# A sequence layer and a product-key expert layer on one core: the one-hots of the second half of a step stand behind the next step's weights, and the turned lists have two buffers

## The chip, the cores and the metric

The kernel runs on one core of one Trainium2 chip. The metric is the device time of one execution in microseconds (us). Five engines work side by side: TensorE (matmuls and transposes, into PSUM), VectorE, ScalarE, GpSimd, and SyncE, which here only starts transfers. Each runs its own instructions in the order in which they are written, and waits for semaphores that the others raise.

## The reference

The input is 4 sequences of 1024 tokens with 128 features. First layer: four projections, softplus, sigmoid and tanh, a scan along the sequence, a gate, an output projection, residual and layer norm. Second layer, cut to what matters here (8 heads, 32 keys, TOPK = 8, 1024 experts):

```python
q = (xn @ w_q.T).reshape(b, n, 2, h, kd).transpose(2, 0, 1, 3, 4)
sim = jnp.einsum('pbnhd,hkpd->pbnhk', q, keys)
s, i = jax.lax.top_k(sim, k)
sx, sy = (s[0], s[1])
ix, iy = (i[0], i[1])
all_scores = (sx[..., :, None] + sy[..., None, :]).reshape(b, n, h, k * k)
all_idx = (ix[..., :, None] * nk + iy[..., None, :]).reshape(b, n, h, k * k)
scores, pk = jax.lax.top_k(all_scores, k)
idx = jnp.take_along_axis(all_idx, pk, axis=-1)
w_down = key_in[idx]
w_up = key_out[idx]
o = jnp.einsum('bnd,bnhkd->bnhk', inputs, w_down)
o = jax.nn.gelu(o, approximate=False) * jax.nn.softmax(scores, axis=-1)
return jnp.einsum('bnhk,bnhkd->bnd', o, w_up)
```

`xn` is a batch norm of `inputs` over all tokens. A residual and a layer norm follow.

## The kernel before

The first layer takes the first fifth of the span and is not touched. The second is a loop of 16 steps (NS) of 256 tokens. It gathers no expert weights. All 1024 experts are evaluated for all tokens by dense matmuls; the weights of the chosen experts are scattered into a dense matrix P (tokens by experts) by small matmuls of one-hots; gelu times P goes through a dense output matmul. The chosen expert is coded as a coarse index of 64 (NI) and a fine index of 16 (NJ).

For the tokens of step m the work is this, by functions:

- `scores(m)` (TensorE, line 837): similarities of two tiles; `sims_out(m)` (ScalarE, line 383) evacuates them, `normed` (line 375) makes the input of a later step.
- `greatest(m)` (VectorE, line 606): the 8 greatest of each row. `candidate_sums(m)` (GpSimd, lines 239 to 248) makes 20 candidate sums and differences. `indices(m)` (VectorE, line 614) finds the indices, `top_sums(m)` (line 620) the 8 greatest candidates. `candidate_codes(m)` and `over_eighth(m)` (GpSimd, lines 253 to 270) make codes and the comparison with the eighth. ScalarE makes exponentials (`exps`, `low_halves`) and signs (`signs`, line 399).
- One step later `pack`, `pick`, `weights_and_codes` (VectorE, lines 627 to 654) pick the 8 codes and weights of the step. `pack` waits for the signs.
- `halves` (GpSimd, lines 277 and 279) splits the weights in a high and a low half in f16, `convert` (ScalarE, line 404) copies the codes. Together they are the four lists.
- `lists_turned(m)` (TensorE, line 844) transposes the lists into a PSUM bank, `lists_out(m)` (ScalarE, line 409) evacuates them to `listsT`.
- `hots_of(m, hf)` (VectorE, lines 666 to 673) makes the one-hots of half `hf` of the step from `listsT` in four instructions, a block of its own for each half. The second is the longest (line 669, 4096 elements a partition).
- `scatter(m, hf)` (TensorE, line 857): 256 small matmuls with their weight loads, from the one-hots of the half; `p_out(m, hf)` (ScalarE, line 417) evacuates the result.
- `weigh(m)` (GpSimd, line 286, four instructions): P times gelu. `experts_in(q)` (TensorE, line 867) and `gelus(q)` (ScalarE, line 423) stand in odd steps only and serve two steps. `experts_out(m)` (TensorE, line 880): the output matmul.
- `residual`, `scales` (VectorE), `spread2`, `norm_out` (ScalarE): the last layer norm of four tiles, once in two steps: `residual` and `spread2` (with a table load for the square root) in odd steps, `scales` and `norm_out` in even ones.

The order on each engine is written out by hand in the loops over m at the end of each block. In iteration m, VectorE runs greatest(m), pack to weights of m - 1, indices(m), top_sums(m), then both blocks of one-hots of m - 1, with `residual` or `scales` between the two. TensorE runs scatter(m - 2, second half), lists_turned(m - 1), scores(m + 1), experts_in in odd steps, scatter(m - 1, first half), experts_out(m - 3). ScalarE follows TensorE: p_out of the second half, lists_out, sims_out, normed, gelus, spread2, signs, norm_out, p_out of the first half. GpSimd runs candidate_sums(m), halves(m - 1), weigh(m - 3), candidate_codes(m), over_eighth(m).

`listsT` is one buffer: lists_out(m) waits until both blocks of one-hots of the step before are done. The functions that the diff touches:

Of the kernel before, what the change touches and what calls it, by code (L numbers as in the profile page):

```python
# [6 lines left out]
ACT = mybir.ActivationFunctionType  # L7
AX_X = mybir.AxisListType.X
F32 = mybir.dt.float32
F16 = mybir.dt.float16  # L10
# [4 lines left out]
P = 128  # L15
# [8 lines left out]
def seqffn_kernel(nc, x, w_in, w_select, w_gate, w_out, w_delta, log_a, gamma, beta, w_q, keys,  # L24
# [16 lines left out]
    NS = T // 2  # L41
# [9 lines left out]
    with ExitStack() as ctx:  # L51
        def sb(name, shape, dt=F32):
            return ctx.enter_context(nc.sbuf_tensor(name, shape, dt))
# [54 lines left out]
        wk = sb("wk", [P, RH, TOPK])  # L108
        codes = sb("codes", [P, 2, 2 * SL], U16)
        lists = sb("lists", [P, 4, 2 * SL], F16)  # L110
        listsT = sb("listsT", [P, 4, P], F16)


        XW, YW = P * NI // 2, P * NJ // 2
# [29 lines left out]
        b_lists = bank(7)[:, 0:256].bitcast(F16)  # L144
# [14 lines left out]
        s = {n: sem(n) for n in names}  # L159
# [5 lines left out]
        def wait(eng, name, value):  # L165
            if value <= 0:
                return
            eng.wait_ge(s[name], value)
# [134 lines left out]
        def _(act):  # L303
# [92 lines left out]
            def signs(m):  # L396
                wait(act, "dt_done", m + 1)
                wait(act, "hi_done", m)
                act.activation(sgn[:, :], above[:, :, :].rearrange("p h c -> p (h c)"), ACT.Sign).then_inc(s["sgn_done"], 1)
# [5 lines left out]

            def lists_out(m):
                wait(act, "lists_mm", m + 1)
                wait(act, "hot_done", m * 2)
                act.activation(listsT[:, :, :].rearrange("p f t -> p (f t)"), b_lists, ACT.Copy).then_inc(s["lists_evac"], 1)  # L409

            def p_out(m, hf):
                wait(act, "p_mm", m * 2 + hf + 1)
# [6 lines left out]
            def gelus(q):  # L419
                wait(act, "y2_mm", q * 2 - 2)  # L420
                for r in range(JR):
                    wait(act, "g_mm", q * JR + (r + 1))
                    act.activation(gl[:, (2 * q) % 4:(2 * q) % 4 + 2, 2 * r:2 * r + 2, :].rearrange("p m j w -> p j m w"),  # L423
                                   b_g[r % 2].rearrange("p (j m w) -> p j m w", j=2, m=2), ACT.Gelu).then_inc(
                                       s["gelu_done"], 1)
# [32 lines left out]
            for m in range(NS + 1):  # L458
                if m < NS:
                    exps(m)  # L460
                if m >= 1:
                    convert(m - 1)
                if m < NS:
                    low_halves(m)
                if m == NS:
                    lists_out(NS - 1)
                if m >= 2:
                    p_out(m - 2, 1)
                if 1 <= m < NS:
                    lists_out(m - 1)  # L470
                if m + 1 < NS:
                    sims_out(m + 1)
                if m + 2 < NS:
                    normed(m + 2)
                if m % 2 and m < NS:
                    gelus(m // 2)
                if m >= 5 and m % 2:
                    spread2(m // 2 - 2)
                if m < NS:
                    signs(m)  # L480
                if m >= 6 and m % 2 == 0:
                    norm_out(m // 2 - 3)
                if m >= 1:
                    p_out(m - 1, 0)
# [8 lines left out]
        def _(dve):  # L493
# [147 lines left out]
            def weights_and_codes(m):  # L641
                wait(dve, "conv_done", m)
                wait(dve, "picked_done", m + 1)
                dve.tensor_copy(exk16, picked16[:, :, :, 0]).then_inc(s["exk_done"], 1)
                dve.tensor_scalar(codes[:, 0, :], picked16[:, 0, :, 1], NE - NJ, None, ALU.bitwise_and)
                wait(dve, "exk_done", m + 1)
                dve.reduce_sum(zsum[:, :], exk[:, :, :], AX_X).then_inc(s["z_done"], 1)
                dve.tensor_scalar(codes[:, 1, :], picked16[:, 0, :, 1], NJ - 1, None,
                                  ALU.bitwise_and).then_inc(s["codes_done"], 1)
                wait(dve, "z_done", m + 1)  # L650
                dve.reciprocal(zinv[:, :], zsum[:, :]).then_inc(s["zinv_done"], 1)
                wait(dve, "zinv_done", m + 1)
                wait(dve, "wlo_done", m)
                dve.scalar_tensor_tensor(out=wk[:, :, :], in0=exk[:, :, :], scalar=W_SCALE,
                                         in1=zinv[:, :].unsqueeze(2).to_broadcast([P, RH, TOPK]), op0=ALU.mult,
                                         op1=ALU.mult).then_inc(s["wk_done"], 1)

            def hots_of(m, hf):
                at = slice(32 * hf, 32 * hf + 32)

                def spread(f, n):
                    v = listsT[:, f, 64 * hf:64 * hf + 64].rearrange("p (g s) -> p g s", s=2)
                    return v.unsqueeze(2).to_broadcast([P, 32, n, 2])

                wait(dve, "lists_evac", m + 1)
                dve.tensor_tensor(hoty[:, at], iota[:, NI:].unsqueeze(1).to_broadcast([P, 32, NJ, 2]),  # L666
                                  spread(1, NJ), ALU.is_equal).then_inc(s["hoty_done"], 1)
                wait(dve, "p_mm", m * 2 - 1 + hf)
                dve.tensor_tensor(hotx[:, at], iota[:, 0:NI].unsqueeze(1).to_broadcast([P, 32, NI, 2]),  # L669
                                  spread(0, NI), ALU.is_equal)  # L670
                wait(dve, "hoty_done", m * 2 + hf + 1)
                dve.tensor_tensor(hotw[:, 0, at], hoty[:, at], spread(2, NJ), ALU.mult)  # L672
                dve.tensor_tensor(hotw[:, 1, at], hoty[:, at], spread(3, NJ), ALU.mult).then_inc(s["hot_done"], 1)  # L673

            def residual(q):
                wait(dve, "out_done", q)
                wait(dve, "y2_mm", q * 2 + 2)
                dve.tensor_tensor(zf.rearrange("p (m e) d -> p m e d", e=2), y2.rearrange("p e m d -> p m e d"),
                                  x1[:, q * CH:(q + 1) * CH, :].rearrange("p (m e) d -> p m e d", e=2),
                                  ALU.add).then_inc(s["zf_done"], 1)  # L680
                wait(dve, "zf_done", q + 1)
                for t in range(CH):
                    end = dve.bn_stats(st2[:, t, :], zf[:, t, :])
                end.then_inc(s["st2_done"], 1)
                wait(dve, "st2_done", q + 1)
                for t in range(CH):
                    end = dve.bn_aggr(mv2[:, t, :], st2[:, t, :])
                end.then_inc(s["mv2_done"], 1)

            def scales(q):  # L690
                wait(dve, "sd2", q + 1)
                dve.reciprocal(rstd2[:, :], rstd2[:, :]).then_inc(s["rstd2_done"], 1)
                wait(dve, "rstd2_done", q + 1)
                dve.scalar_tensor_tensor(out=nmr2[:, :], in0=mv2[:, :, 0], scalar=-1.0, in1=rstd2[:, :],
                                         op0=ALU.mult, op1=ALU.mult).then_inc(s["nmr2_done"], 1)

            for m in range(NS + 1):
                if m < NS:
                    greatest(m)
                if m >= 1:  # L700
                    pack(m - 1)
                    pick(m - 1)
                    weights_and_codes(m - 1)
                if m < NS:
                    indices(m)
                    top_sums(m)
                if m >= 1:
                    hots_of(m - 1, 0)
                    if m >= 5 and m % 2:
                        residual(m // 2 - 2)  # L710
                    if m >= 6 and m % 2 == 0:
                        scales(m // 2 - 3)
                    hots_of(m - 1, 1)

            def last_residual(u):
                n = slice(2 * u, 2 * u + 2)
# [36 lines left out]
        def _(pe):  # L753
# [64 lines left out]
            for r in range(ROWS):  # L818
                p, h = r // H, r % H
# [63 lines left out]

            scores(0)
            for m in range(NS + 1):
                if m == NS:
                    lists_turned(NS - 1)
                if m >= 2:
                    scatter(m - 2, 1)
                if 1 <= m < NS:  # L890
                    lists_turned(m - 1)
                if m + 1 < NS:
                    scores(m + 1)
                if m % 2 and m < NS:
                    experts_in(m // 2)
                if m == NS:
                    wait(pe, "lists_evac", NS)
                    experts_out(NS - 3)
                if m >= 1:
                    scatter(m - 1, 0)  # L900
                if 3 <= m < NS:
                    wait(pe, "lists_evac", m)
                    experts_out(m - 3)
# [28 lines left out]
```

## Time and profile before

| | |
|---|---|
| median of 3 runs | 532.36 us (530.75 to 534.48) |
| the profiled execution | 531.46 us, span 529.7 us |
| mean granted TensorE clock | 0.768 |
| PE (TensorE matmuls) busy | 369.5 us, 70% |
| DVE (VectorE) busy | 444.1 us, 84% |
| ACT (ScalarE) busy | 236.2 us, 45% |
| POOL (GpSimd) busy | 220.0 us, 42% |
| the chain that ended last, by engine | PE 52%, DVE 20%, issue 17%, ACT 8% |

The span is what the trace covers; the execution's own time is 1.8 us longer. PE stands for TensorE's matmuls and PEld for its weight loads, which overlap them. The chain is followed back from the last instruction, at each step to what released it. "issue" is time in which an engine waited for nothing that the profile shows.

### The profile page before, as it was taken

Reading aid. Unit: us, or ns where it says so; the run is one execution under the profiler, and the core shown is the slowest. Engines: PE = TensorE matmul, PEld = TensorE weight load, DVE = VectorE, ACT = ScalarE, POOL = GpSimd, SP = SyncE. Lnnn points to the kernel's source line nnn. Section 1 sums busy time; section 2 is a strip of 40 time slices with the busy share of each in tenths; the row PEclk is TensorE's granted clock in tenths of the full one; section 3 lists DMA queues with packets and bytes.
Section 4 is the critical chain, followed back from the end, with each engine's and each line's share of the span. In section 5 each row is a group of like instructions: output and inputs, shape, how many; then the busy total and the mean of one; then the engine's idle time right before and its main releaser. Section 6 shows DMA issues by size and latency. Waiting matters only on the chain.

```text
span 529.7 us, 24223 instructions
## 1 busy us (share of the span) xinstructions
PE 369.5 (70%) x10097; PEld 270.4 (51%) x10097; DVE 444.1 (84%) x2770; ACT 236.2 (45%) x371; POOL 220.0 (42%) x311
## 2 busy tenths in 40 slices
PE   5686786418537775786777787847976876778856
PEld 2233474114434555464736484726464656556855
DVE  1537899699999969898999699989998997998643
ACT  3967804426514532463346235632644372345212
POOL 1042420144348751616283428435252747082630
PEclk9989965759655876898778668876886796588878
DMA  8700000000000000000000000000000000000001
GB/s 236 165 0 2 1 1 0 1 1 2 4 2 5 3 2 4 3 4 4 24 2 4 4 24 3 4 22 5 2 5 24 5 3 4 22 4 2 24 6 41
DMA packets 7661, 8.95 MB, mean 17 GB/s; under 512 B 896, under 2 KB 6912, under 8 KB 7424
## 3 DMA queue, kind: packets, MB, share of 16 engines
q1 hardware_dynamic: 6976, 7.34, 5.1%
q8 instruction: 79, 1.29, 1.0%
q14 instruction: 30, 0.25, 0.1%
q10 hardware_dynamic: 576, 0.07, 0.1%
HBM read 5.31 MB, written 2.10 MB: 14 GB/s over the span
## 4 chain that ended last, share of the span: by engine, by line
PE 52%; DVE 20%; issue 17%; ACT 8%; DMA 1%; SPq 0%; ACTq 0%; DVEq 0%
PE psum L880 17%; PE psum L857 16%; PE psum L867 9%; PE psum L837 5%; PE psum L776 4%; DVE arena L669 3%; DVE idx L614 3%; DVE arena L525 2%; DVE x L575 2%; ACT L423 1%; DVE vals L606 1%; DVE arena L673 1%; DVE arena L666 1%; DVE arena L672 1%; DVE picked L638 1%
## 5 line engine op out<-in xcount | busy, mean ns | idle before, releaser
L857 PE MATMUL psum<-arena 64*64 64x16 f16 x8192 | 93.8, 182 | 91.5 <-issue 70.0
L857 PEld LDWEIGHTS psum<-arena 64*64 64x64 f16 x8192 | 87.7, 120 | 110.0 <-issue 104.8
L880 PE MATMUL psum<-ko,arena 64*128 64x128 f32 x1024 | 91.2, 355 | 3.6 <-issue 3.6
L417 ACT ACTIVATE arena<-psum 128x1024 f32<-128x1024 f32 x32 | 32.8, 1024 | 134.0 <-PE psum L857 134.0
L880 PEld LDWEIGHTS psum<-ko,arena 64*128 64x128 f32 x1024 | 88.0, 267 | 4.2 <-issue 3.9
L239 POOL TENSOR_TENSOR cand<-vals 128x128 f32<-128x128 f32 x16 | 13.2, 824 | 169.1 <-DVE vals L606 169.1
L614 DVE FIND_INDEX8 idx<-vals,sims 128x8 uint32<-128x32 f32 x512 | 82.7, 185 | 0.0
L286 POOL TENSOR_TENSOR arena<-arena 128x512 f32<-128x512 f32 x60 | 77.8, 1331 | 4.2 <-ACT arena L417 4.2
L669 DVE TENSOR_TENSOR arena<-iota,listsT 128x4096 f16<-128x4096 f16 x32 | 74.9, 2341 | 0.0
L867 PE MATMUL psum<-x1T,trn 128*64 128x256 f32 x512 | 62.8, 400 | 8.7 <-ACT arena L423 8.7
L837 PE MATMUL psum<-msim,xn 128*128 128x512 f32 x64 | 54.9, 1008 | 4.9 <-ACT xn L375 4.9
L867 PEld LDWEIGHTS psum<-x1T,trn 128*64 128x64 f32 x512 | 33.9, 143 | 43.9 <-ACT arena L423 20.7
L606 DVE MAX8 vals<-sims 128x8 f32<-128x32 f32 x512 | 49.1, 173 | 3.7 <-ACT sims L383 3.5
L666 DVE TENSOR_TENSOR arena<-iota,listsT 128x1024 f16<-128x1024 f16 x32 | 23.2, 724 | 26.6 <-ACT listsT L409 26.6
L423 ACT ACTIVATE arena<-psum 128x512 f32<-128x512 f32 x64 | 37.4, 597 | 17.2 <-PE psum L867 17.1
L638 DVE MAX8 picked<-words 128x8 f32<-128x20 f32 x512 | 42.8, 165 | 1.7
L776 PE MATMUL psum<-arena,trn 128*128 128x512 f32 x64 | 34.6, 674 | 10.1 <-ACT arena L343 8.8
L614 DVE MATCH_VALUE_LOAD idx<-vals,sims 128x8 f32 x512 | 36.8, 72 | 0.0
L383 ACT ACTIVATE sims<-psum 128x512 f32<-128x512 f32 x32 | 19.0, 596 | 27.6 <-PE psum L837 27.5
L259 POOL TENSOR_TENSOR code<-ixf,iyf 128x128 f32<-128x128 f32 x16 | 30.3, 1891 | 1.3
L837 PEld LDWEIGHTS psum<-msim,xn 128*128 128x128 f32 x64 | 17.6, 301 | 22.3 <-issue 19.5
L776 PEld LDWEIGHTS psum<-arena,trn 128*128 128x128 f32 x64 | 12.2, 215 | 26.5 <-issue 18.6
(113 smaller groups left out, 529.5 us busy)
## 6 DMA issues: line engine op xcount, KB each, us to landing
x<-in_L_attn_x_dram SPq DMA_DIRECT2D x8, 256.0 KB, 4.7
out_dram<-nat SPq DMA_DIRECT2D x7, 256.0 KB, 2.3
ko<-in_L_ffn_key_out_dram SPq DMA_DIRECT2D x2, 512.0 KB, 9.5
nat<-in_L_ffn_key_in_dram SPq DMA_DIRECT2D x2, 256.0 KB, 8.0
nat<-in_L_ffn_keys_dram SPq DMA_DIRECT2D x2, 128.0 KB, 5.4
out_dram<-nat SPq DMA_DIRECT2D x2, 128.0 KB, 1.7
nat<-in_L_attn_W_delta_dram SPq DMA_DIRECT2D x1, 64.0 KB, 2.8
nat<-in_L_attn_W_in_dram SPq DMA_DIRECT2D x1, 64.0 KB, 2.7
```

The lines of the kernel that those rows point to most:

```text
L286: pool.tensor_tensor(gl[:, m % 4, js], pn[:, m % 3, js], gl[:, m % 4, js], ALU.mult).then_inc(s["a_done"], 1)
L417: act.activation(dst, src, ACT.Copy, scale=1.0 / W_SCALE).then_inc(s["p_evac"], 1)
L423: act.activation(gl[:, (2 * q) % 4:(2 * q) % 4 + 2, 2 * r:2 * r + 2, :].rearrange("p m j w -> p j m w"), b_g[r % 2].rearrange("p (j m w) - ...
L606: end = dve.max(vals[:, p, t * H + h, :], sims[:, m % 2, t, r, :])
L614: end = dve.max_index(idx[:, p, t * H + h, :], vals[:, p, t * H + h, :], sims[:, m % 2, t, r, :])
L638: end = dve.max(picked[:, w, r, :], words[:, w, r, :])
L669: dve.tensor_tensor(hotx[:, at], iota[:, 0:NI].unsqueeze(1).to_broadcast([P, 32, NI, 2]), spread(0, NI), ALU.is_equal)
L776: pe.matmul(to, trn[:, n, :], xT[:, k], start=True, stop=True).then_inc(s[done], 1)
L837: pe.matmul(b_sim[t], xn[:, t], msim[:, :], start=True, stop=True).then_inc(s["sim_mm"], 1)
L857: end = pe.matmul(psum[64 * e:64 * e + 64, at:at + NJ], hotx[rows, g, :, e], hotw[rows, part, g, :, e], start=(part == 0), stop=(part == 1))
L867: end = pe.matmul(b_g[r % 2][64 * e:64 * e + 64, b * SW:(b + 1) * SW], trn[:, 9 + r, 64 * b:64 * b + 64], tokens[:, e], start=True, stop=True)
L880: end = pe.matmul(y2[:, e, m % 2] if m < NS - 1 else y_last[:, e], gl[rows, m % 4, j, :], ko[rows, j, :], start=(j == 0), stop=(j == NJ - 1))
```

## The change

VectorE's second block of one-hots of a step moves: it now stands one iteration later, behind pack, pick and weights of the following step and ahead of indices. `scales` stands behind it, `residual` behind the first block. TensorE turns the lists ahead of the second-half scatter, ScalarE evacuates the lists ahead of that scatter's result. `listsT` gets two buffers, so that lists_out(m) waits only for the one-hots of step m - 2. On ScalarE the signs stand ahead of `spread2`.

```diff
-        listsT = sb("listsT", [P, 4, P], F16)
+        listsT = sb("listsT", [P, 2, 4, P], F16)
...
             def lists_out(m):
                 wait(act, "lists_mm", m + 1)
-                wait(act, "hot_done", m * 2)
-                act.activation(listsT[:, :, :].rearrange("p f t -> p (f t)"), b_lists, ACT.Copy).then_inc(s["lists_evac"], 1)
+                wait(act, "hot_done", (m - 1) * 2)
+                act.activation(listsT[:, m % 2].rearrange("p f t -> p (f t)"), b_lists, ACT.Copy).then_inc(s["lists_evac"], 1)
...
                 if m < NS:
                     low_halves(m)
-                if m == NS:
-                    lists_out(NS - 1)
+                if m >= 1:
+                    lists_out(m - 1)
                 if m >= 2:
                     p_out(m - 2, 1)
-                if 1 <= m < NS:
-                    lists_out(m - 1)
                 if m + 1 < NS:
                     sims_out(m + 1)
                 if m + 2 < NS:
                     normed(m + 2)
                 if m % 2 and m < NS:
                     gelus(m // 2)
+                if m < NS:
+                    signs(m)
                 if m >= 5 and m % 2:
                     spread2(m // 2 - 2)
-                if m < NS:
-                    signs(m)
...
-                    v = listsT[:, f, 64 * hf:64 * hf + 64].rearrange("p (g s) -> p g s", s=2)
+                    v = listsT[:, m % 2, f, 64 * hf:64 * hf + 64].rearrange("p (g s) -> p g s", s=2)
...
                     pack(m - 1)
                     pick(m - 1)
                     weights_and_codes(m - 1)
+                if m >= 2:
+                    hots_of(m - 2, 1)
+                if m >= 6 and m % 2 == 0:
+                    scales(m // 2 - 3)
                 if m < NS:
                     indices(m)
                     top_sums(m)
                 if m >= 1:
                     hots_of(m - 1, 0)
-                    if m >= 5 and m % 2:
-                        residual(m // 2 - 2)
-                    if m >= 6 and m % 2 == 0:
-                        scales(m // 2 - 3)
-                    hots_of(m - 1, 1)
+                if m >= 5 and m % 2:
+                    residual(m // 2 - 2)
+            hots_of(NS - 1, 1)
...
             for m in range(NS + 1):
-                if m == NS:
-                    lists_turned(NS - 1)
+                if m >= 1:
+                    lists_turned(m - 1)
                 if m >= 2:
                     scatter(m - 2, 1)
-                if 1 <= m < NS:
-                    lists_turned(m - 1)
                 if m + 1 < NS:
                     scores(m + 1)
```

## Rows read from the trace of the kernel before

**Rows 1.** Waits: engine and line, waited for: us in total, times, longest us.
```profile
DVE arena L666 <- ACT listsT L409: 26.6, 9, 5.1
...
PE psum L857 <- DVE arena L673: 18.0, 7, 6.0
```

**Rows 2.** Timeline of TensorE: start us, us, work, [idle before and releaser]; pairs' ends.
```profile
150.49 2.05 PE L857 MATMUL psum<-arena 64*64 64x16 f16 x130 [5.97 <-DVE arena L673]
...
169.72 1.45 PE L867 MATMUL psum<-x1T,trn 128*64 128x256 f32 x6
...
178.38 1.72 PE L857 MATMUL psum<-arena 64*64 64x16 f16 x184
...
481.37 1.77 PE L857 MATMUL psum<-arena 64*64 64x16 f16 x190
```

**Rows 3.** Timeline of TensorE, one pair of steps, 333 to 384 us.
```profile
333.31 1.72 PE L857 MATMUL psum<-arena 64*64 64x16 f16 x185
...
353.67 1.09 PE L857 MATMUL psum<-arena 64*64 64x16 f16 x110 [2.46 <-DVE arena L673]
357.02 1.89 PE L857 MATMUL psum<-arena 64*64 64x16 f16 x128 [2.26 <-issue]
...
366.81 1.62 PE L857 MATMUL psum<-arena 64*64 64x16 f16 x173
...
371.50 0.40 PE L844 MATMUL psum<-ident,lists 128*128 128x128 f16 x4
...
383.80 0.37 PE L857 MATMUL psum<-arena 64*64 64x16 f16 x23
```

**Rows 4.** Timeline of ScalarE in the same pair.
```profile
333.43 0.60 ACT L423 ACTIVATE arena<-psum 128x512 f32<-128x512 f32 x1 [0.27 <-PE psum L867]
...
335.54 0.45 ACT L399 ACTIVATE sgn<-above 128x320 f32<-128x320 f32 x1
...
347.86 1.02 ACT L417 ACTIVATE arena<-psum 128x1024 f32<-128x1024 f32 x1 [5.91 <-PE psum L857]
348.78 0.59 ACT L409 ACTIVATE listsT<-psum 128x512 f16<-128x512 f16 x1
```

**Rows 5.** Timeline of VectorE in the same pair.
```profile
336.08 0.94 DVE L627 SCALAR_TENSOR_TENSOR words<-sgn,code 128x640 uint16<-128x640 f32 x1 [0.28 <-issue]
...
340.88 0.29 DVE L654 SCALAR_TENSOR_TENSOR wk<-exk,zinv 128x128 f32<-128x128 f32 x1
...
346.25 1.37 DVE L620 MAX8 top<-cand 128x8 f32<-128x20 f32 x16
349.40 0.72 DVE L666 TENSOR_TENSOR arena<-iota,listsT 128x1024 f16<-128x1024 f16 x1 [1.79 <-ACT listsT L409]
...
353.72 0.69 DVE L666 TENSOR_TENSOR arena<-iota,listsT 128x1024 f16<-128x1024 f16 x1
...
357.73 3.07 DVE L606 MAX8 vals<-sims 128x8 f32<-128x32 f32 x32
360.72 0.87 DVE L627 SCALAR_TENSOR_TENSOR words<-sgn,code 128x640 uint16<-128x640 f32 x1
```

**Rows 6.** Timeline of GpSimd in the same pair, behind the weights.
```profile
341.30 0.29 POOL L277 CAST lists<-wk 128x128 f16<-128x128 f32 x1 [2.77 <-DVE wk L654]
341.67 0.43 POOL L279 TENSOR_TENSOR lists<-wk,lists 128x128 f16<-128x128 f32 x1
342.06 4.95 POOL L286 TENSOR_TENSOR arena<-arena 128x512 f32<-128x512 f32 x4
```

**Rows 7.** Timelines of VectorE and GpSimd, start-up and a later odd step.
```profile
122.15 0.76 DVE L666 TENSOR_TENSOR arena<-iota,listsT 128x1024 f16<-128x1024 f16 x1
...
123.05 2.36 POOL L264 TENSOR_TENSOR code<-ixf,iyf 128x64 f32<-128x64 f32 x1
...
127.05 0.68 DVE L666 TENSOR_TENSOR arena<-iota,listsT 128x1024 f16<-128x1024 f16 x1
...
270.05 4.31 POOL L259 TENSOR_TENSOR code<-ixf,iyf 128x128 f32<-128x128 f32 x1
```

## The prediction

> **What bounds the kernel now.** I read the busy shares first, then the waits, then the timeline of each engine over one pair of steps. VectorE is busy for 84% of the span, but the waits name only one real hole in it: 26.6 us in nine waits of line 666 for the turned lists [rows 1]. TensorE waits 18.0 us in seven waits for a finished hot block (line 673) [rows 1]; one of them, 5.97 us, is in the start-up [rows 2], so the other six are 2.0 us each.
>
> The step loop repeats in pairs, because the expert matmuls (line 867) and their gelus stand only in odd steps. The first scatter after them starts at 178.38 us in the first full pair and at 481.37 us in the last [rows 2]: six pairs in 303.0 us, 50.5 us each. I take the pair from 333.31 to 383.80 (50.49 us) as the pattern [rows 3]. In it two rings can be seen:
>
> - TensorE's ring: the second-half scatter starts at 366.81, the turning of the lists only follows at 371.50 [rows 3]. ScalarE must then first empty the scatter (347.86) and only after that the lists (348.78) [rows 4], so VectorE begins the next first half 1.79 us late, at 349.40 [rows 5], and TensorE waits for it until 353.67 [rows 3]. This is what the change goes for.
> - VectorE's ring has almost no slack: the last gelu of the pair starts at 333.43 and the signs, behind the square root, at 335.54 [rows 4]; pack starts at 336.08 [rows 5].
>
> TensorE without its one 2.0 us wait would need 48.5 us a pair, so nothing that only frees VectorE can give more than about 2.0 x 6 + 6.0 = 18 us.
>
> **What the change removes.** The lists are turned ahead of the second-half scatter and evacuated ahead of p_out, and a second buffer lets that happen while the old lists are still read. The lists then stand ready well before indices and top sums end, so the wait of line 666 goes: I cost the list waits at 0 after the change (the cover is 6.5 us of indices and top sums). The signs no longer stand behind the square root and its table load: pack may start 1.2 us after the expert matmuls end instead of 2.77 us (0.1 us to the last gelu, 0.6 us of it, 0.5 us as now between signs and pack: 333.43, 335.54, 336.08 against 333.31) [rows 3 to 5]. The second buffer itself issues nothing. No DMA moves.
>
> **What the change adds.** The second-half block of one step now stands between the next step's weights and its indices, and its scatter comes directly after it. Everything that TensorE does after the lists waits for that block. The new ring, from the end of the expert matmuls to the end of the next, by the durations of the rows:
>
> 1. gelu and signs: 1.2 us.
> 2. pack, pick, weights: 336.08 to 341.1 (line 654 starts at 340.88, 0.2 us between starts) [rows 5]: 5.0 us.
> 3. second-half block: 353.72 to 357.73 = 4.0 us when undisturbed [rows 5].
> 4. scales: 0.3 us (the gap between the two blocks beyond 4.0).
> 5. indices and top sums: 341.1 to 347.55 (346.25 + 1.37, less 0.07 overlap) [rows 5]: 6.45 us.
> 6. first-half block: 4.0 us undisturbed.
> 7. greatest: 357.73 to 360.72 = 3.0 us [rows 5]; its similarities are there, since their matmuls run beside the block of point 6.
> 8. pack, pick, weights again: 4.95 us.
> 9. second-half block again: 4.0 us; to TensorE 0.1 us.
> 10. scatter, similarities, expert matmuls: 366.81 to 383.80 [rows 3] = 17.0 us.
>
> The sum is 50.0 us, against 50.5 us now. So even with every block undisturbed the ring only changes its shape: the 2 us that TensorE loses today at line 857 it goes on losing, because points 1 to 6 (21.0 us) reach the first-half scatter later than 353.67 - 333.31 = 20.36 us [rows 3]. VectorE's freed time turns into a wait at pack: its own work is about 47.3 us a pair (50.5 less its waits of about 3), and the ring holds it at signs for the rest.
>
> **The price of the neighbours.** The blocks will not be undisturbed. Now the second-half block runs while GpSimd waits. After the change it starts 0.2 us after line 654 starts, while GpSimd starts line 277 at 0.42 us (341.30 against 340.88), then line 279, then four products of 4.95 us together [rows 5, 6]. What such neighbours do is seen in the start-up: a first-half block from 122.15 took 4.9 us to the next block's start at 127.05 instead of 4.0, and line 264 of GpSimd took 2.36 us beside line 669 [rows 7]. In the other pattern GpSimd gets nothing until the block is over: line 259 took 4.31 us from 270.05 [rows 7]. The Trainium skill, "Trainium Architecture — The Big Picture", "What this means for kernel authors", says that VectorE and GpSimd share a port pair under an exclusive lock, not a split bandwidth. By that rule alone the block would stay at 4.0 us and GpSimd's halves would come after it; the trace has that pattern in rows 7, and also the one in which VectorE pays.
>
> Bounds per pair. Lowest: nobody is disturbed, 50.0 us. GpSimd held: the halves (0.3 + 0.4 us and their gaps) and the turned lists (0.4 us) come after the block, in front of its scatter, +1.4 us in point 9: 51.4 us. VectorE disturbed: the product behind the halves is longer (4.95 / 4 = 1.24 us) than the line of the start-up, so a second-half block may reach 5.4 us, and the first-half one 4.9 us: 53.7 us. I take 4.9 us for the second-half blocks, the measured disturbed block, and half of its surplus for the first-half one (GpSimd's codes are delayed by the products and overlap it in part): 50.0 + 0.9 + 0.9 + 0.45 = 52.25 us, that is +1.75 x 6 = +10.5 us over the six pairs.
>
> **Start-up.** The first-half block of step 1 is done at 150.4 now and then too, as VectorE has no wait there. Greatest, weights and the second-half block follow: 150.4 + 3.0 + 4.95 + 4.9 = 163.3, then scatter and similarities of 4.7 + 3.7 us: 171.7, where the expert matmuls now start at 169.72 [rows 2]. With half a microsecond for the disturbed block of step 0: +2.5 us. **Tail.** After 481.37 the weights of the last step and the moved block end 1.2 + 5.0 + 4.9 = 11.1 us later; TensorE reached that scatter 11.9 us later, so 0.
>
> Sum: 531.46 us of the profiled execution + 10.5 + 2.5 = 544.5 us. The median shown is 0.9 us above that execution, so 545 us.
>
> **The rivals.**
>
> - *Nothing to see.* GpSimd gives way cheaply, or the disturbed blocks fall where TensorE is late anyway (the first-half scatter from 353.67 and the experts' output together take 13.1 us, more than the 12.0 us of points 7 to 9). Then -0.5 x 6 + 1 to +0.7 x 6: 530 to 537 us. For it: several pairs have such long scatters. Against it: point 9 is the wait of TensorE in all others.
> - *Faster.* TensorE's scatters hold issue gaps, as the 2.26 us before 357.02 [rows 3], that no engine causes. If the new wait in front of the second-half scatter lets the instructions gather, point 10 shrinks by up to 2.0 us, and with undisturbed blocks a pair takes 48.0 to 49.5 us: -1 to -2.5 a pair, 517 to 526 us. It decides from 49.6 us a pair down. Against it: this very scatter follows a wait of 2.46 us and still gets no further than 110 matmuls before its gap [rows 3].
> - *The halves held and the block undisturbed*, 51.4 us a pair: +5.4 + 2 = 539 us. It is the lower end of my own case.
>
> **Chances.** One per cent, about what can be told from no change, is 5.3 us. My case (new ring, disturbed by GpSimd), 538 to 556 us: 0.61. Nothing to see: 0.25. Faster: 0.14. The range reaches from inside the faster case, 527, to the full disturbed sum: 53.7 us gives +19 us and +3.5 us at the start, 554; I end it at 555. My own case has the range 538 to 555. Faster by over 1%: 0.14; within 1%: 0.25; slower: 0.61.
>
> **What would show it.** Line 666 no longer waits for line 409. Line 627 waits about 2 us in every even step, and what ended that wait is the sign of line 399, right behind the last gelu. TensorE waits for line 673 twice a pair, at both scatters, in all some 25 to 35 us instead of 18.0. Line 279 grows from 0.43 us to over 1 us, or lines 666 to 673 from 4.0 to about 4.9 us a block. A pair takes 52 us. I am wrong if pairs fall under 50 us; then either pack does not wait for the gelus or point 10 is shorter than 17.0 us.

## The result: 566.15 us, slower by 6.6%

The changed kernel takes 566.15 us (median of 4 runs, 564.82 to 567.88) against 533.36 us of the kernel before beside it; the ratio is 1.0657, 95% interval 1.0602 to 1.0713. It was forecast slower, but 545 us and at most 555. The new ring that was forecast is there, but the price put on GpSimd's neighbourhood in it, and on the start, was too low.

### The profile after

Shares of the page after (busy us, share of the span of 566.1 us, instructions):

```profile
PE 379.6 (67%) x10097; PEld 277.9 (49%) x10097; DVE 482.1 (85%) x2770; ACT 235.9 (42%) x371; POOL 280.4 (50%) x311
```

VectorE has the same instructions and is busy 38 us longer, GpSimd 60 us longer. So the same work takes longer, which no wait for a semaphore shows. On GpSimd alone that need not cost time: in e1 below it is busy 267.3 us at the time of the kernel before. The waits after (engine, line, waited for: us in total, times, longest):

```profile
ACT listsT L409 <- PE psum L844: 47.4, 16, 4.8
...
PE psum L857 <- DVE arena L671: 38.6, 17, 4.2
...
DVE words L625 <- issue: 25.7, 7, 7.0
```

VectorE's wait for the turned lists [rows 1] has gone from the list. In its place VectorE waits at pack (line 625, "issue", 25.7 us in 7 waits), and TensorE's waits for a finished block went from 18.0 us in 7 to 38.6 us in 17.

One pair of steps on TensorE after, which answers to [rows 3]. Lines above 600 on VectorE stand two lower after the change: line 671 is line 673 of the kernel before, 667 is 669.

```profile
352.92 1.72 PE L857 MATMUL psum<-arena 64*64 64x16 f16 x185
...
363.16 0.40 PE L844 MATMUL psum<-ident,lists 128*128 128x128 f16 x4
364.70 2.19 PE L857 MATMUL psum<-arena 64*64 64x16 f16 x243 [1.14 <-DVE arena L671]
...
377.17 1.67 PE L857 MATMUL psum<-arena 64*64 64x16 f16 x110 [4.10 <-DVE arena L671]
```

TensorE now waits at both scatters of the even step. Its pairs end at 186.89, 240.20, 295.15, 352.92, 407.04, 462.05 and 516.54 us: 54.9 us each, where it was 50.5 [rows 2]. VectorE in the same pair, which answers to [rows 5]:

```profile
354.08 0.92 DVE L625 SCALAR_TENSOR_TENSOR words<-sgn,code 128x640 uint16<-128x640 f32 x1 [5.38 <-issue]
...
359.06 0.69 DVE L664 TENSOR_TENSOR arena<-iota,listsT 128x1024 f16<-128x1024 f16 x1
359.66 2.38 DVE L667 TENSOR_TENSOR arena<-iota,listsT 128x4096 f16<-128x4096 f16 x1
361.96 0.91 DVE L670 TENSOR_TENSOR arena<-arena,listsT 128x1024 f16<-128x1024 f16 x1
362.80 1.75 DVE L671 TENSOR_TENSOR arena<-arena,listsT 128x1024 f16<-128x1024 f16 x1
364.47 0.17 DVE L690 RECIPROCAL rstd<-rstd 128x4 f32<-128x4 f32 x1
364.67 1.02 DVE L692 SCALAR_TENSOR_TENSOR nmr<-mv,rstd 128x4 f32<-128x4 f32 x1
...
372.06 0.75 DVE L664 TENSOR_TENSOR arena<-iota,listsT 128x1024 f16<-128x1024 f16 x1
...
375.79 1.23 DVE L671 TENSOR_TENSOR arena<-arena,listsT 128x1024 f16<-128x1024 f16 x1
376.95 3.06 DVE L604 MAX8 vals<-sims 128x8 f32<-128x32 f32 x32
```

And GpSimd beside it, which answers to [rows 6]:

```profile
359.28 0.62 POOL L277 CAST lists<-wk 128x128 f16<-128x128 f32 x1 [8.44 <-DVE wk L652]
359.98 2.35 POOL L279 TENSOR_TENSOR lists<-wk,lists 128x128 f16<-128x128 f32 x1
362.29 5.84 POOL L286 TENSOR_TENSOR arena<-arena 128x512 f32<-128x512 f32 x4
```

I read this as the two engines taking turns. Line 279 (0.43 us before) ends 0.3 us after line 667; line 671 (0.68 us undisturbed) takes 1.75 us while the first product of line 286 runs; and line 692, four elements a partition, takes 1.02 us instead of 0.16 beside the next product. That the products do this to line 671 is tested in e4. The second-half block takes 5.41 us (359.06 to 364.47), the scales 1.15 us with their gaps (to 365.62), the first-half block 4.89 us (372.06 to 376.95). From block to block these lengths repeat within 0.03 us, in every step from 3 to 14.

### The profile page after: what moved, and what is told of

The parts are those of the page before. It is cut to its first block, busy times and chain, and to the rows that moved or that the text cites. A ratio compares the mean times of both kernels' runs of the same rounds, so it can differ in the third digit from the quotient of the medians.

```text
span 566.1 us, 24222 instructions
## 1 busy us (share of the span) xinstructions
PE 379.6 (67%) x10097; PEld 277.9 (49%) x10097; DVE 482.1 (85%) x2770; ACT 235.9 (42%) x371; POOL 280.4 (50%) x311
## 4 chain that ended last, share of the span: by engine, by line
DVE 47%; PE 28%; issue 15%; ACT 8%; DMA 1%; SPq 0%; DVEq 0%; POOL 0%; ACTq 0%
DVE idx L612 7%; PE psum L857 7%; DVE picked L636 7%; DVE arena L667 5%; DVE arena L671 5%; PE psum L837 5%; PE psum L880 5%; PE psum L867 5%; DVE vals L604 4%; PE psum L776 4%; DVE arena L670 3%; DVE arena L664 2%; DVE words L625 2%; DVE arena L523 2%; DVE top L618 2%
## 5 line engine op out<-in xcount | busy, mean ns | idle before, releaser
L857 PE MATMUL psum<-arena 64*64 64x16 f16 x8192 | 99.2, 185 | 110.6 <-issue 70.6
L857 PEld LDWEIGHTS psum<-arena 64*64 64x64 f16 x8192 | 93.3, 125 | 130.3 <-issue 128.3
L286 POOL TENSOR_TENSOR arena<-arena 128x512 f32<-128x512 f32 x60 | 92.7, 1575 | 0.0
L880 PE MATMUL psum<-ko,arena 64*128 64x128 f32 x1024 | 90.2, 353 | 3.2 <-issue 3.2
L667 DVE TENSOR_TENSOR arena<-iota,listsT 128x4096 f16<-128x4096 f16 x32 | 78.4, 2450 | 0.0
L239 POOL TENSOR_TENSOR cand<-vals 128x128 f32<-128x128 f32 x16 | 11.6, 723 | 92.3 <-DVE vals L604 92.3
L867 PEld LDWEIGHTS psum<-x1T,trn 128*64 128x64 f32 x512 | 33.9, 143 | 43.3 <-ACT arena L423 20.4
L671 DVE TENSOR_TENSOR arena<-arena,listsT 128x1024 f16<-128x1024 f16 x32 | 46.1, 1442 | 0.0
L277 POOL CAST lists<-wk 128x128 f16<-128x128 f32 x16 | 9.3, 581 | 73.6 <-DVE wk L652 73.6
L423 ACT ACTIVATE arena<-psum 128x512 f32<-128x512 f32 x64 | 37.4, 597 | 17.5 <-PE psum L867 17.4
L776 PE MATMUL psum<-arena,trn 128*128 128x512 f32 x64 | 36.0, 699 | 10.1 <-ACT arena L343 8.8
L279 POOL TENSOR_TENSOR lists<-wk,lists 128x128 f16<-128x128 f32 x16 | 35.7, 2231 | 1.3
L625 DVE SCALAR_TENSOR_TENSOR words<-sgn,code 128x640 uint16<-128x640 f32 x16 | 14.3, 895 | 25.7 <-issue 25.7
L264 POOL TENSOR_TENSOR code<-ixf,iyf 128x64 f32<-128x64 f32 x16 | 35.8, 2236 | 0.0
## 6 DMA issues: line engine op xcount, KB each, us to landing
ko<-in_L_ffn_key_out_dram SPq DMA_DIRECT2D x2, 512.0 KB, 10.1
```

Source lines behind the costliest of these rows:

```text
L286: pool.tensor_tensor(gl[:, m % 4, js], pn[:, m % 3, js], gl[:, m % 4, js], ALU.mult).then_inc(s["a_done"], 1)
L776: pe.matmul(to, trn[:, n, :], xT[:, k], start=True, stop=True).then_inc(s[done], 1)
L857: end = pe.matmul(psum[64 * e:64 * e + 64, at:at + NJ], hotx[rows, g, :, e], hotw[rows, part, g, :, e], start=(part == 0), stop=(part == 1))
L867: end = pe.matmul(b_g[r % 2][64 * e:64 * e + 64, b * SW:(b + 1) * SW], trn[:, 9 + r, 64 * b:64 * b + 64], tokens[:, e], start=True, stop=True)
L880: end = pe.matmul(y2[:, e, m % 2] if m < NS - 1 else y_last[:, e], gl[rows, m % 4, j, :], ko[rows, j, :], start=(j == 0), stop=(j == NJ - 1))
```

## The experiments

Each ratio is to the kernel before, run beside it on the same chip. "Pair" is the mean of the six pairs, read as in [rows 2]; the second and the last end are given where the start matters.

**e1: the lists' part alone.** Edits to the kernel before: `listsT` doubled and `lists_out` with the changed wait, and on TensorE (on ScalarE alike)

```diff
-                if m == NS:
-                    lists_turned(NS - 1)
+                if m >= 1:
+                    lists_turned(m - 1)
                 if m >= 2:
                     scatter(m - 2, 1)
-                if 1 <= m < NS:
-                    lists_turned(m - 1)
```

> The part of the change that concerns the lists, alone: two buffers, lists turned ahead of the second-half scatter and evacuated ahead of its result; both blocks of one-hots stay together on VectorE, the signs stay behind the square root. Theory (the new ring through the moved block is guilty, the lists' part is good): line 666 no longer waits for the lists (26.6 us before), a pair of steps falls from 50.5 to 48.5 to 49.5 us, 519 to 527 us in all. Rival (TensorE's new order is itself the cost): 545 us or more. Rival (the freed wait only moves): 530 to 535 us.

533.34 us, ratio 1.0021 (0.9981 to 1.0061): no difference. But the pairs fell to 49.55 us, and VectorE's waits for the lists from 26.6 us in nine to one of 3.2 us; 5 us were lost ahead of the pairs. TensorE in iteration 3 of e1:

```profile
154.43 1.88 PE L855 MATMUL psum<-arena 64*64 64x16 f16 x126 [1.84 <-issue]
163.33 0.79 PE L842 MATMUL psum<-ident,lists 128*128 128x128 f16 x4 [7.02 <-issue]
164.05 1.88 PE L855 MATMUL psum<-arena 64*64 64x16 f16 x125
```

The scatter at 164.05 had its one-hots long before, but stands behind the lists of the next step, which VectorE had not made yet. Before, it began at 157.7 us. The forecast "545 us or more" for TensorE's order falls; so does my 519 to 527.

**e2: the moved block alone**, lists and signs as before, one buffer.

```diff
                     weights_and_codes(m - 1)
+                if m >= 2:
+                    hots_of(m - 2, 1)
+                if m >= 6 and m % 2 == 0:
+                    scales(m // 2 - 3)
...
-                    hots_of(m - 1, 1)
+            hots_of(NS - 1, 1)
```

> The other part alone: the second-half block stands behind the next step's weights (scales behind it, residual behind the first block); one buffer for the turned lists, the old order of lists, scatter and signs on TensorE and ScalarE. Theory: the moved block makes the ring, so this is at least as slow as the whole change, 563 to 575 us, with a pair at 54.5 to 56.5 us. Rival (the order of the lists and of the signs is guilty): 530 to 540 us.

578.92 us, ratio 1.0884 (1.0826 to 1.0942), pair 56.75 us. The move alone costs 47 us; the lists' and the signs' part give 12 us of that back in the whole change. The move is the guilty part. With one buffer and the old order VectorE also waits for the lists here, 10.1 us in seven waits.

**e3: the ring cut.** The changed kernel with the signs ahead of the gelus on ScalarE:

```diff
+                if m < NS:
+                    signs(m)
                 if m % 2 and m < NS:
                     gelus(m // 2)
-                if m < NS:
-                    signs(m)
```

> The changed kernel with the signs of a step ahead of its gelus on ScalarE, so that pack of the next step no longer waits for the expert matmuls. Theory (a ring gelus, signs, pack, block, ..., block, scatter, expert matmuls of 54.9 us): the ring is cut, VectorE's wait of about 5 us at pack goes, a pair takes what VectorE's own work takes, 49.5 to 51.5 us, and the whole 533 to 546 us. Rival (TensorE's waits and lower clock, or the port between VectorE and GpSimd by itself, make the time): above 558 us.

553.08 us, ratio 1.0388 (1.0342 to 1.0433), between theory and rival. The line of pack's waits is gone, as the theory has it, but the pair takes 52.8 us and the start lost 7 us: the gelus of step 1 had to wait for its signs, and the first pair began at 138.35 instead of 131.63 us. By the second pair some 2 us of that are left: from the first similarities to it e3 takes 91.1 us, the changed kernel 88.7, and e11, which takes this fault out, 89.0.

**e4: the products held.** The changed kernel with

```diff
                 if m >= 3:
+                    wait(pool, "hot_done", (m - 1) * 2)
                     weigh(m - 3)
```

> The changed kernel with one wait more on GpSimd: the four products of weigh start only when the second-half block that stands beside them is done. Theory (GpSimd's products lengthen the block, twice in the ring): line 671 falls from 1.75 us to 1.25 or less in the second-half blocks, the block from 5.4 to 4.4 to 4.9 us, a pair by 1 to 2 us, the whole to 552 to 561 us. Rival (the lengthening costs nothing, since something else is late): 564 to 568 us.

556.00 us, ratio 1.0466 (1.04 to 1.0532), pair 53.5 us: as the theory says, with the block a little shorter than it had it. A second-half block of e4:

```profile
349.36 0.68 DVE L665 TENSOR_TENSOR arena<-iota,listsT 128x1024 f16<-128x1024 f16 x1
349.96 2.38 DVE L668 TENSOR_TENSOR arena<-iota,listsT 128x4096 f16<-128x4096 f16 x1
352.26 0.91 DVE L671 TENSOR_TENSOR arena<-arena,listsT 128x1024 f16<-128x1024 f16 x1
353.09 0.68 DVE L672 TENSOR_TENSOR arena<-arena,listsT 128x1024 f16<-128x1024 f16 x1
```

The last instruction (line 672 here, 671 of the changed kernel) is back at 0.68 us, and the block is 4.34 us. Adding a wait made the changed kernel 10 us faster.

**e7: line 279 left out too** (the low halves of the weights are set to zero once, and what waited for line 279 waits for line 277), products held as in e4.

```diff
                 pool.tensor_copy(lists[:, 2, :], flat).then_inc(s["whi_done"], 1)
-                wait(pool, "whi_done", m + 1)
-                pool.tensor_tensor(lists[:, 3, :], flat, lists[:, 2, :], ALU.subtract).then_inc(s["wlo_done"], 1)
```

> The changed kernel with GpSimd's neighbours of the second-half block nearly taken away: line 279 is left out (the low halves of the weights are zero, so the weights are coarser), and weigh waits for the block. Theory (GpSimd's access beside the block lengthens it from 4.0 to 5.4 us, twice a ring): block 4.0 to 4.3 us, pair 52 to 53 us, whole 544 to 554 us. Rival (e4 took all that there is to take): 555 to 558 us.

550.58 us, ratio 1.04 (1.0331 to 1.047), pair 53.2 us, just above the range given. The total lies in its range, but its ratio is not clear of e4's (1.0466), so that leaving out line 279 gains more time is not shown; its block shows what line 279 did. Every instruction but one has the undisturbed length:

```profile
347.18 0.69 DVE L664 TENSOR_TENSOR arena<-iota,listsT 128x1024 f16<-128x1024 f16 x1
347.78 2.38 DVE L667 TENSOR_TENSOR arena<-iota,listsT 128x4096 f16<-128x4096 f16 x1
350.08 0.68 DVE L670 TENSOR_TENSOR arena<-arena,listsT 128x1024 f16<-128x1024 f16 x1
350.69 0.68 DVE L671 TENSOR_TENSOR arena<-arena,listsT 128x1024 f16<-128x1024 f16 x1
351.29 0.16 DVE L690 RECIPROCAL rstd<-rstd 128x4 f32<-128x4 f32 x1
351.48 1.25 DVE L692 SCALAR_TENSOR_TENSOR nmr<-mv,rstd 128x4 f32<-128x4 f32 x1
```

The block is 4.10 us; the products, now released right there, meet the scales instead (1.25 us).

**e8: e3 and e4 together**, both edits as above.

> The changed kernel with the edits of e3 and e4 together: signs ahead of the gelus, products held until the block is done. Theory (two causes that add: the ring is worth 2.2 us a pair and the products 1.4 us a pair): VectorE without waits, pair 51 to 52 us, whole 539 to 549 us. Rival (the two hide each other): the time of e3, 550 to 555 us.

541.48 us, ratio 1.022 (1.0159 to 1.0281), pair 50.6 us. The two causes add: 2.7% (e3) and 1.9% (e4), 4.4% together. The start has the fault of e3 (first pair from 139.34 us).

**e11 and e10: the signs first from iteration 3 on**, in e11 alone, in e10 with the products held.

```diff
+                if 3 <= m < NS:
+                    signs(m)
                 if m % 2 and m < NS:
                     gelus(m // 2)
-                if m < NS:
+                if m < 3:
                     signs(m)
```

> The changed kernel with the signs first from iteration 3 on and nothing else: the ring cut, the neighbours on the port left. Theory: pairs of 52.8 us as in e3, 541 to 547 us; against the changed kernel's 566 us the ring is worth 19 to 25 us, the rest is VectorE's own lengthened work. Rival (e3's time was not that of its start): 550 us or more.

e11: 547.82 us, ratio 1.0282 (1.0229 to 1.0336), pair 52.2 us; the median is 0.8 us above the range given, far from the rival.

> The changed kernel with both edits of e8, the signs first only from iteration 3 on (in e3 and e8 the first gelus waited for the signs of step 1 and the first scatter behind the expert matmuls began 9 us late). Theory (ring and port together are the whole loss): pairs of 50.5 us as in e8, 529 to 536 us, no more than 1% over before. Rival (something else costs too): 538 us or more.

e10: 540.50 us, ratio 1.0155 (1.0103 to 1.0208), pair 50.7 us. The pairs came as expected, the total did not: the rival's number holds. Of its 8 us over the kernel before, the trace has 1 us in the six pairs, 1 us behind them and 5.3 us ahead of them: the second pair starts at 183.64, where it was 178.38 [rows 2].

**e5 and e6: more of the lists' part.** e5 has e1's edits with the old order up to iteration 2, e6 the signs ahead of the gelus as well.

> The lists' part alone as in e1, but the first three iterations keep the old order (in e1 the second scatter of step 1 stood behind the lists of step 2 and began at 164.1 instead of 157.7 us, and the expert matmuls 5 us later). Theory: the 5 us of the start-up come back and the pairs of 49.5 us stay (50.5 before), 524 to 529 us. Rival (the shorter pairs of e1 were paid for by the late start, the work only spreads): 531 to 534 us.

> As e5, and the signs of a step ahead of its gelus on ScalarE. Theory: pack's waits (21.5 us in e1) go, VectorE is ready sooner and TensorE, with 48.5 us of its own a pair, is the only bound: 519 to 526 us. Rival (TensorE bounds already, VectorE's wait costs nothing): the time of e5 within 2 us.

e5: 532.21 us, ratio 1.0029 (0.999 to 1.0067). I had put the border one iteration too early: the late scatter stands in iteration 3, and the first pair again took 54.1 us. e6: 540.81 us, ratio 1.0193 (1.0132 to 1.0253), pair 49.5 us as in e5, and the gelus of step 1 late. Pack's waits (22.1 us in e5) went, and VectorE waited for the lists instead (36.3 us in 8 waits): in this order of VectorE the time of a pair does not go through pack. What e6 lost, it lost at the start.

**e9: the lists early from iteration 4 on**, the blocks where they were.

```diff
+                if m >= 4:
+                    lists_turned(m - 1)
                 if m >= 2:
                     scatter(m - 2, 1)
-                if 1 <= m < NS:
+                if 1 <= m < 4:
                     lists_turned(m - 1)
```

> The lists' part alone, early from iteration 4 on instead of 3 (e5 still had the late scatter of step 1, which stands in iteration 3: its first pair took 54.1 us, 49.4 before). Theory: the start-up is that of before and the six pairs stay at 49.5 us (50.5 before): 523 to 528 us, 1% under before. Rival (TensorE bounds, and what the pairs gain at the start of the loop goes back): 529 to 533 us.

526.91 us, ratio 0.992 (0.9885 to 0.9954): 0.8% faster than the kernel before, a small gain, but its interval is clear of 1. Pair 49.7 us, first pair 48.5. Here the lists go ahead and the scatter behind them waits for nobody:

```profile
336.10 0.40 PE L844 MATMUL psum<-ident,lists 128*128 128x128 f16 x4
336.42 2.52 PE L857 MATMUL psum<-arena 64*64 64x16 f16 x243
...
341.75 3.78 PE L837 MATMUL psum<-msim,xn 128*128 128x512 f32 x4
345.46 1.67 PE L857 MATMUL psum<-arena 64*64 64x16 f16 x110
```

The first-half scatter at 345.46, 19.3 us behind the expert matmuls (326.20), has no wait where the kernel before had 2.46 us and 20.4 us [rows 3]. In all of e9 TensorE waits for a block once:

```profile
PE psum L857 <- DVE arena L673: 6.5, 1, 6.5
```

**e12: the signs' part alone**, signs ahead of spread2 in the kernel before.

> The third part of the change alone: the kernel before with the signs ahead of spread2 on ScalarE. Theory (in the kernel before TensorE and the lists set the pair, pack has slack behind it): pack starts 1.6 us earlier in even steps, the wait of line 666 for the lists grows by as much, and the time stays, 528 to 536 us. Rival (pack is on the path there too): 1.6 us off each of 6 pairs, 520 to 525 us.

530.44 us, ratio 0.9994 (0.9944 to 1.0044): no difference, as expected. The waits for the lists did not grow (22.1 us in 8 here), so that detail of the theory is not borne out.

## Why the prediction was wrong

**Right: what it does.** The waits for the lists went; pack waits for the signs behind the last gelu (354.08 against 352.92, 1.16 us where I had 1.2); TensorE waits at both scatters (38.6 us in all, where I had 25 to 35). e3, e8 and e11 show that the ring exists: with it cut, pack's waits are gone and the ratio falls from 1.0657 to 1.0282, 3.75% or 20 us. e4 shows that GpSimd beside the second-half blocks lengthens them and that this reaches the end. e2 shows that it is the moved block and not the order of the lists.

**Argued, not shown: the bare ring costs nothing.** Points 1 to 10 with undisturbed blocks gave 50.0 us. No run has the ring without GpSimd beside it: e7 comes nearest, with 53.2 us a pair, and still has the first-half block at 4.88 us and the scales at 1.37. What can be checked are the pieces. Measured pieces of the same ring in the pair from 352.92 to 407.04, in the order of the points: 1.16, 4.98, 5.41, 1.15, 6.44, 4.89, 2.98, 4.90, 5.42, 0.35, 16.44, sum 54.1 us. Every piece on VectorE that meets none of GpSimd's long instructions is within 0.06 us of what I had; the last two, TensorE's, are 0.25 us more and 0.6 us less in this pair.

**Wrong: the step "The price of the neighbours".** It is a matter of size: the forecast has this cost, and too little of it. I took 4.9 us for the second-half blocks and half of the surplus for the first-half one, a middle between bounds, and had the whole reason for the upper bound in hand: the product behind the halves is 1.24 us long and must be let through. Measured, with what it was short by in a pair:

- second-half block 5.41 us, not 4.9: 2 x 0.5 = 1.0 us;
- first-half block 4.89 us, not 4.45: 0.45 us; GpSimd's codes start when the indices are done and always meet it;
- scales 1.15 us, not 0.3: 0.85 us, in none of the bounds. I had costed the moved line of four elements by its length without neighbours, though it too has two inputs in SBUF and stands beside the products;
- point 10, scatter to the end of the expert matmuls: 17.5 us in the mean of six (16.4 to 20.3), not 17.0: 0.5 us. The chosen pair was a fast one: in the kernel before the mean of six was already 17.3 us.

52.25 + 2.8 = 55.0 us; measured 54.9. Over six pairs I forecast +10.5 us; it was +26.7.

The whole price was in the trace before, in its last block, which the forecast did not use. There a block met the products of line 286 and took 7.24 us (499.15 to 506.39), up to 1.1 us more for one instruction:

```profile
498.27 0.68 DVE L673 TENSOR_TENSOR arena<-arena,listsT 128x1024 f16<-128x1024 f16 x1
...
499.06 0.16 DVE L694 SCALAR_TENSOR_TENSOR nmr<-mv,rstd 128x4 f32<-128x4 f32 x1
499.15 0.68 DVE L666 TENSOR_TENSOR arena<-iota,listsT 128x1024 f16<-128x1024 f16 x1
499.75 3.37 DVE L669 TENSOR_TENSOR arena<-iota,listsT 128x4096 f16<-128x4096 f16 x1
503.04 1.76 DVE L672 TENSOR_TENSOR arena<-arena,listsT 128x1024 f16<-128x1024 f16 x1
504.72 1.75 DVE L673 TENSOR_TENSOR arena<-arena,listsT 128x1024 f16<-128x1024 f16 x1
```

```profile
499.15 8.44 POOL L286 TENSOR_TENSOR arena<-arena 128x512 f32<-128x512 f32 x4 [4.16 <-ACT arena L417]
```

**TensorE's clock is not the cause.** The mean granted clock over the six pairs was 0.73 after and 0.77 before, so e3's rival has to be weighed. TensorE was busy 229.7 us in them after and 225.0 us before, so a slower clock can account for about 4.6 of the 26.7 us at most; and e4, with 0.78, still has pairs of 53.5 us. The issue gaps in the scatters are the same in both kernels, 70.0 us before and 70.6 after.

**Wrong: the start.** Forecast +2.5 us. The second pair starts at 186.89 instead of 178.38; 2.7 us of that stand ahead of the loop (the first similarities at 98.23 instead of 95.55 us), where nothing was changed and other runs differ by as much (94.9 to 98.7 us). That leaves 5.8 us. The scatter of step 1 began at 166.90, 0.9 us later than my 163.3 + 2.7, and then took 7.7 us instead of the 4.7 us that I had from the chosen pair (it shows no wait for an engine, only issue gaps; in the kernel before this same scatter took 6.1 us). The runs say more. From the first similarities to the second pair it is 82.8 us before, 88.7 after, 87.9 with the lists' part alone (e1), 90.2 with the moved block alone (e2) and 82.0 in e9, which turns the lists early from iteration 4 on. So the one part alone costs 5 us at the start and the other 7, and they do not add; the whole change with e9's late border was not run, so how much the early lists make in it is open.

**Wrong: the tail**, costed at 0: TensorE waits 1.18 us for the moved block after the last pair, and the tail is 1.2 us longer. The trace adds up: 2.7 + 5.8 + 26.7 + 1.2 = 36.4 us, the difference of the two spans.

**The range.** I ended it at 555 us with an upper sum of 53.7 us that left out the scales and took point 10 from one pair. With both in, the same sum is 55.0 us a pair, and with the 3.5 us that I allowed for the start about 563 us, still 3 us short of the result. The rest is the start and the tail.

**The rivals.** "Nothing to see": the long first-half scatters did cover part of the ring in single pairs (in the pair shown TensorE ended its output matmul at 390.28, VectorE its block at 390.25), but in the mean did not help. "Faster", by issue gaps filled during the new waits: false; the scatters behind the waits still took 4.4 to 8.0 us. "Halves held and the block undisturbed": not seen once after the change.

**The rule on the port.** By the Trainium skill ("Trainium Architecture — The Big Picture", "What this means for kernel authors") VectorE and GpSimd share a port pair under an exclusive lock, not a split bandwidth. I had read it as if VectorE would then keep the port for a whole block of four instructions. The trace agrees with a lock that is passed on between single instructions: line 671 grew from 0.68 to 1.75 us beside a product. Where GpSimd's instruction starts 0.2 us after the block, it is let in between two of VectorE's; in [rows 7] line 259, which starts 0.06 us after its block (269.99 us), got nothing for 4.31 us. No run tells what decides between the two.

**TensorE's bound.** I had 48.5 us a pair for TensorE without waits. e9 removes them and takes 49.7 us; so about 1 us of the 2.0 us wait came back in another form. The mean granted clock is nearly the same (0.764 in e9, 0.768 before); the cause is open.

## What to carry to other kernels

- Before an instruction is moved, look at what GpSimd does in the place where it goes, not only at the waits: here VectorE's instructions with two inputs in SBUF and GpSimd's made each other longer, by up to the neighbour's whole instruction, and a tiny instruction paid as much as a long one.
- When the middle of a block is taken out and put in front of another chain, follow the whole ring once around through every engine (here gelu, signs, pack, block, scatter, expert matmuls) and take the measured length of every piece at its new neighbours. And take the parts of a change apart: here the moved block was worth +8.8%, and the early lists nothing as they stood and -0.8% from iteration 4 on.
- In an order written by hand the first iterations are a case of their own. Early lists paid from iteration 4 on and cost 5 us in iteration 3; signs ahead of gelus in iteration 1 put the first scatter behind the expert matmuls 7 us or more later.

## What was not expected of the hardware

- A wait added on GpSimd (e4) took 10 us off the changed kernel: VectorE's line 671 fell from 1.75 to 0.68 us in the second-half blocks of the pairs.
- A VectorE instruction with four elements a partition (line 692) took 0.90 us in the mean of 7 (0.16 before): 1.02 us beside a product that was under way, and 1.25 us in e7, where the product started with it. The reciprocal just ahead of it (line 690) stayed at 0.17 us.
- GpSimd's one-input cast (line 277) grew as well: 0.62 us beside line 664, 0.29 us alone.
